# A conv-attention-MLP block on one core: pass 1 of the feed-forward part with its bias on TensorE, maxima taken from PSUM, and the normalisation on GpSimd

## The reference, cut to what matters

```python
def _quantize_activations_groupwise(x):      # 5 groups of 32 // 5 = 6 images, the last 2 images stay zero
    for g in range(5):
        ag = x[g * gs:(g + 1) * gs]
        gamma = jnp.max(jnp.abs(ag))
        xq = xq.at[g * gs:(g + 1) * gs].set(jnp.clip(ag * 128 / (gamma + 1e-5), -128 + 1e-5, 128 - 1e-5))
def _bitlinear(x, W, b):
    y = jnp.einsum('btc,oc->bto', x, binarized(W)) + b
    return _quantize_activations_groupwise(y)
h = _bitlinear(ln(t), W1, b1)                # 192 -> 768
out = _bitlinear(gelu(h), W2, b2)            # 768 -> 192
t = t + out
```

## Time and profile before

| | |
|---|---|
| time, median of 3 runs | 4890.53 us (4886.1 to 4891.87) |
| the profiled execution's own time | 4894.14 us |
| its span in the trace | 4892.3 us |
| PE busy | 4119.3 us (84% of the span) |
| DVE busy | 3418.6 us (70%) |
| ACT busy | 2759.7 us (56%) |
| POOL busy | 359.1 us (7%) |
| pass 1 of group 0: first statistics to last maximum | 785.92 to 895.42 us, 109.5 us |
| in it: PE, DVE, ACT, POOL busy | 75.84, 77.71, 58.63, 31.28 us |

### The profile page before, as it was taken

One profiled execution on the slowest core, in us unless ns is written; L12 is line 12 of the kernel. 1 busy time (PEld: TensorE's weight loads), 2 busy tenths in 40 slices (PEclk: granted clock), 3 DMA queues, 4 the chain that ended last, 5 costly groups with the idle time before them and its releaser, 6 DMA issues.

```text
span 4892.3 us, 114220 instructions
## 1 busy us (share of the span) xinstructions
PE 4119.3 (84%) x38848; PEld 2965.8 (61%) x38848; DVE 3418.6 (70%) x6624; ACT 2759.7 (56%) x5791; POOL 359.1 (7%) x311
## 2 busy tenths in 40 slices
PE   3989897879898878989887879889878989887878
PEld 2766664566676636766664566666536667664565
DVE  3767677777676667767677777676677767676776
ACT  1555555646565555555555655555565555565655
POOL 0000002000000120000002000000120000002000
PEclk8999998999999989999998999999989999998999
DMA  2111111011121101111111011121101111111011
GB/s 60 40 34 34 34 40 27 0 47 34 34 54 40 34 0 39 34 34 34 35 40 27 0 47 34 41 53 34 34 0 40 34 34 34 40 34 27 0 40 40
DMA packets 46377, 161.59 MB, mean 33 GB/s; under 512 B 10098, under 2 KB 10612, under 8 KB 45684
## 3 DMA queue, kind: packets, MB, share of 16 engines
q1 hardware_dynamic: 45812, 154.38, 13.3%
HBM read 28.52 MB, written 25.17 MB: 11 GB/s over the span
## 4 chain that ended last, share of the span: by engine, by line
issue 76%; PE 13%; POOL 6%; DVE 2%; ACT 2%; DMA 0%; POOLq 0%; SPq 0%; ACTq 0%; DVEq 0%
PE S L685 5%; PE PT L754 4%; POOL hi_z L478 2%; POOL hi_z L497 1%; POOL rstd L473 1%; POOL rstd L493 1%; ACT work L908 1%; POOL NK L468 1%; PE PT L649 1%; PE OUT L669 1%; DVE work L364 0%; DVE nmax L1103 0%; DMA B<-in_b 0%; PE S L635 0%; PE S L693 0%
## 5 line engine op out<-in xcount | busy, mean ns | idle before, releaser
L863 ACT ACTIVATE work<-S,nmax 128x256 f32<-128x256 f32 (+7 forms) x1536 | 1141.4, 744 | 1113.6 <-DVE nmax L1103 1048.5
L1103 DVE TENSOR_REDUCE nmax<-S 128x1 f32<-128x256 f32 (+7 forms) x1536 | 1157.4, 754 | 845.8 <-PE S L637 830.0
L649 PE MATMUL PT<-ident,work 128*128 128x128 f32 x6912 | 1112.7, 281 | 214.2 <-DVE work L364 184.4
L649 PEld LDWEIGHTS PT<-ident,work 128*128 128x128 f32 x6912 | 748.0, 142 | 430.5 <-DVE work L364 260.4
L364 DVE COPY work<-PT 128x512 f32<-128x512 f32 (+3 forms) x1536 | 893.5, 583 | 57.4 <-PE PT L649 52.3
L685 PE MATMUL S<-odd,W1b 128*128 (+1 forms) x2160 | 567.2, 419 | 96.0 <-ACT work L908 47.0
L685 PEld LDWEIGHTS S<-odd,W1b 128*128 128x128 f16 x2160 | 215.2, 106 | 419.8 <-issue 148.6
L635 PE MATMUL S<-KS,QS 128*128 128x512 f16 (+3 forms) x1152 | 333.1, 345 | 105.7 <-issue 57.0
L867 ACT ACTIVATE work<-PT 128x512 f32<-128x512 f32 (+3 forms) x768 | 331.8, 432 | 53.4 <-PE PT L649 53.4
L637 PE MATMUL S<-causal,identb 128*128 128x128 bf16 x1536 | 342.4, 223 | 0.0
L635 PE MATMUL S<-odd 128*128 128x512 f16 (+3 forms) x1152 | 315.1, 328 | 16.9 <-ACT work L863 14.8
(11 more groups left out here) (183 smaller groups left out, 5760.9 us busy)
## 6 DMA issues: line engine op xcount, KB each, us to landing
X<-in_x SPq DMA_DIRECT2D x32, 768.0 KB, 5.4
odd<-hi_z SPq DMA_DIRECT2D x128, 192.0 KB, 4.3
odd<-odd SPq DMA_DIRECT2D x128, 192.0 KB, 4.3
out_y<-work SPq DMA_DIRECT2D x64, 384.0 KB, 3.7
QS<-hi_z SPq DMA_DIRECT2D x64, 192.0 KB, 3.7
QS<-odd SPq DMA_DIRECT2D x64, 192.0 KB, 4.2
KS<-hi_z SPq DMA_DIRECT2D x64, 192.0 KB, 4.7
KS<-odd SPq DMA_DIRECT2D x64, 192.0 KB, 4.6
```

Of the source, the lines that this page charges most:

```text
L649: last = tr(bank[:, P * (j - c0):P * (j - c0) + P], PS[m % 2][:, m // 2 % 2, P * j:P * j + P], ident[:, :])
L863: A(PS[n % 2][:, n // 2 % 2, 0:w], S[:, n % 2, 0:w], ACT.Exp, bias=nmax[:, n % MAXES:n % MAXES + 1], accum_out=rowsum[:, sum_col(n):sum_co ...
L1103: v.tensor_reduce(nmax[:, n % MAXES:n % MAXES + 1], S[:, n % 2, 0:P * (qtile(n) + 1)], AX.X, ALU.max, negate=True).then_inc(max_made, 1)
```

## The change

In pass 1 only:

1. **Bias on TensorE.** The bias is cut once, in the setup, into three bf16 parts whose sum is the fp32 value; they stand in rows 0, 64 and 96 of an otherwise zero 128x768 array `B1S` (three DMAs of 768 single elements each into rows of `BF`, a view of `T1`; three operations of VectorE make the parts after image 0's front). Each product of 512 columns now starts with one more matmul, `B1S` against a bf16 column of ones read 512 times, and the three products add to it.
2. **Maximum of absolute values straight from PSUM.** VectorE reads the 1024 columns of `S` itself, with the absolute value applied; ScalarE's L891 and the array `JUNK` are gone, and TensorE waits for VectorE's maximum of block m-2 before it writes block m.
3. **Transposes between the tiles.** The four steps of `turn_z2(b + 1)` stand behind blocks 1, 2, 3 and 4 of `y1(b)`.
4. **Normalisation on GpSimd, rounding on ScalarE.** GpSimd does the eight subtract-and-scale operations of 128x192 (L510 of the new file), ScalarE the two roundings of 128x768 (`round_z2`), GpSimd again the two low parts. VectorE keeps the statistics and makes them two images ahead: those of image b+2 between the maxima of image b.

```diff
+            BF = T1[:, GS - 1, 0:4, :].rearrange("p t c -> p (t c)")
...
+            for row in (0, 64, 96):
+                sp.dma_start(BF[row:row + 1, :].rearrange("r (m p) -> r m p", m=MH), b1.rearrange("p m -> m p").unsqueeze(0),
+                             allow_slow_non_contiguous=True).then_inc(bias_parts_in, 16)
...  # GpSimd
-                with pool.Fori(0, GS) as b:
-                    ab = pool.snap(g * GS + b)
-                    pool.wait_ge(ln2_step, ab * LN_PER + 16)
+                for b in range(GS):
+                    ab = g * GS + b
+                    pool.wait_ge(ln2_step, ab * 16 + 16)
                     pool.tensor_tensor(rstd[:, :], mv[:, :, 1], epst[:, :], ALU.add).then_inc(rstd2_made, 1)
                     pool.wait_ge(rstd2_made, ab * 2 + 1)
                     pool.tensor_tensor(rstd[:, :], rstd[:, :], halfneg[:, 0:TT], ALU.pow).then_inc(rstd2_made, 1)
+                    pool.wait_ge(rstd2_made, ab * 2 + 2)
+                    alone(pool)
                     for hf in range(2):
-                        pool.wait_ge(ln2_step, ab * LN_PER + (25 + hf))
+                        pool.wait_ge(z2_rounded, ab * 2 + (hf + 1))
+                        alone(pool)
+                        for t in range(4 * hf, 4 * hf + 4):
+                            pool.tensor_scalar(Z[:, t, :], T1[:, b, t, :], mv[:, t, 0:1], rstd[:, t:t + 1], ALU.subtract,
+                                               ALU.mult).then_inc(z2_normed, 1)
+                    for hf in range(2):
+                        pool.wait_ge(z2_rounded, ab * 2 + (hf + 3))
                         ts = slice(4 * hf, 4 * hf + 4)
                         pool.tensor_tensor(zcat[:, ts, C:2 * C], Z[:, ts, :], zcat[:, ts, 0:C],
                                            ALU.subtract).then_inc(z2lo_made, 1)
...  # TensorE
-                        pe.wait_ge(abs_made, ab * MH + (m + 1))
+                        pe.wait_ge(max1_step, ab * MH + g + (m + MH - 1))
+                        alone(pe)
                         for hf in range(2):
-                            last = ffn1(Z2[:, b, hf], S[:, m % 2, 512 * hf:512 * hf + 512], m)
+                            bank = S[:, m % 2, 512 * hf:512 * hf + 512]
+                            mm(bank, B1S[:, P * m:P * m + P], onesb[:, :].broadcast_to([P, 512]), start=True, stop=False)
+                            for j in range(3):
+                                last = mm(bank, W1b[:, j, P * m:P * m + P], Z2[:, b, hf, j, :], start=False, stop=(j == 2))
                         last.then_inc(y1_full, 1)
+                        if ab1 is not None and 1 <= m <= 4:
+                            turn_z2(ab1, m - 1)
...  # ScalarE
+                def round_z2(ab):
+                    act.wait_ge(z2t_full, ab * 4 + 4)
+                    for hf in range(2):
+                        act.wait_ge(z2_normed, ab * 8 + (4 * hf + 12))
+                        alone(act)
+                        A(zcat[:, 4 * hf:4 * hf + 4, 0:C], Z[:, 4 * hf:4 * hf + 4, :], ACT.Copy).then_inc(z2_rounded, 1)
...
-                        A(JUNK[:, m, :], S[:, m % 2, :], ACT.Abs, bias=B1[:, m:m + 1]).then_inc(abs_made, 1)
...
+                with act.Fori(0, GS) as b:
+                    ab = act.snap(g * GS + b)
+                    round_z2(ab)
+                    put_z2(b, ab)
...  # VectorE, setup
+            dve.wait_ge(bias_parts_in, 48)
+            tops = BF.bitcast(BF16).rearrange("p (n two) -> p n two", two=2)[:, :, 1]
+            link(v.tensor_tensor(BF[64:P, :], BF[64:P, :], tops[64:P, :], ALU.subtract))
+            link(v.tensor_tensor(BF[96:P, :], BF[96:P, :], tops[96:P, :], ALU.subtract))
+            link(v.tensor_copy(B1S[:, :], tops))
...  # VectorE, pass 1
-                        v.tensor_reduce(gm1[:, b, m:m + 1], JUNK[:, m, :], AX.X, ALU.max).then_inc(max1_step, 1)
...
+                def aggregate2(ab):
+
+                    dve.wait_ge(z2_normed, ab * 8 + 8)
+                    dve.wait_ge(ln2_step, ab * 16 + 8)
...
+                    v.tensor_reduce(gm1[:, b, m:m + 1], S[:, m % 2, :], AX.X, ALU.max,
+                                    apply_absolute_value=True).then_inc(max1_step, 1)
...
+                with dve.Fori(0, GS - 2) as b:
                     ab = dve.snap(g * GS + b)
...
+                    for m in range(MH):
+                        max_y1(b, ab, m)
+                        if m == 1:
+                            dve.wait_ge(ln2_step, ab * 16 + 32)
+                            alone(dve)
+                        if 1 <= m <= 2:
+                            stats2(dve.snap(b + 2), range(4 * m - 4, 4 * m))
+                        if m == 3:
+                            aggregate2(dve.snap(ab + 2))
```

More of the change, by code:

```diff
@@ L303, in hybrid_kernel @@
         y1_full = sem("y1_full")
[L304 removed]
+        z2_normed = sem("z2_normed")
+        z2_rounded = sem("z2_rounded")
+        bias_parts_in = sem("bias_parts_in")
         max1_step = sem("max1_step")
@@ L707, in group_tail, with turn_z2, y1 @@
                 alone(pe)
[L709 to L717, removed]
+                def turn_z2(ab, k):
+                    if k % 2 == 0:
+                        pe.wait_ge(z2lo_made, ab * 2 + (k // 2 + 1))
+                    if k >= 2:
+                        pe.wait_ge(z2t_made, ab * 4 + (k - 1))
+                    turn_z(ZP[k % 2], k).then_inc(z2t_full, 1)
+                def y1(b, ab, ab1):
                     for m in range(MH):
@@ L885, in put_z2 @@
                           ACT.Copy).then_inc(z2t_made, 1)
-                def abs_y1(ab):
-                    for m in range(MH):
-                        act.wait_ge(y1_full, ab * MH + (m + 1))
-                        act.wait_ge(max1_step, ab * MH + g + (m + 1))
-                        A(JUNK[:, m, :], S[:, m % 2, :], ACT.Abs, bias=B1[:, m:m + 1]).then_inc(abs_made, 1)
-                put_z2(0, g * GS)
-                with act.Fori(0, GS - 1) as b:
+                with act.Fori(0, GS) as b:
                     ab = act.snap(g * GS + b)
-                    abs_y1(ab)
-                    put_z2(act.snap(b + 1), act.snap(ab + 1))
-                abs_y1(g * GS + (GS - 1))
+                    round_z2(ab)
+                    put_z2(b, ab)
                 act.wait_ge(quant1_step, (g + 1) * 4)
@@ L1121, in group_tail @@
                     dve.wait_ge(st, nb * (GS * STACKS) + STACKS)
-                def norm2(b, ab, part, tiles):
-                    layer_norm(lambda t: T1[:, b, t, :], ln2_step, ab * LN_PER, rstd2_made, ab * 2 + 2, part, tiles)
-                def max_y1(b, ab, ms):
-                    for m in ms:
-                        dve.wait_ge(abs_made, ab * MH + (m + 3))
-                        v.tensor_reduce(gm1[:, b, m:m + 1], JUNK[:, m, :], AX.X, ALU.max).then_inc(max1_step, 1)
-                halves = (range(4), range(4, 8))
@@ L1132, in group_tail @@
-                for part, tiles in (("stats", range(TT)), ("norm", range(TT)), ("round", halves[0]), ("round", halves[1])):
-                    norm2(0, g * GS, part, tiles)
-                with dve.Fori(0, GS - 1) as b:
-                    ab = dve.snap(g * GS + b)
-                    b1, ab1 = dve.snap(b + 1), dve.snap(ab + 1)
-                    norm2(b1, ab1, "stats", range(TT))
-                    max_y1(b, ab, range(2))
-                    dve.wait_ge(z2t_full, ab * 4 + 4)
-                    alone(dve)
-                    norm2(b1, ab1, "norm", range(TT))
-                    norm2(b1, ab1, "round", halves[0])
-                    norm2(b1, ab1, "round", halves[1])
-                    max_y1(b, ab, range(2, MH))
@@ L1146, in group_tail, with stats2 @@
-                max_y1(GS - 1, g * GS + (GS - 1), range(MH))
+                def stats2(b, tiles):
+                    for t in tiles:
+                        v.bn_stats(stats[:, t, :], T1[:, b, t, :]).then_inc(ln2_step, 1)
+                def aggregate2(ab):
+                    dve.wait_ge(z2_normed, ab * 8 + 8)
+                    dve.wait_ge(ln2_step, ab * 16 + 8)
+                    alone(dve)
+                    for t in range(TT):
+                        v.bn_aggr(mv[:, t, :], stats[:, t, :]).then_inc(ln2_step, 1)
@@ new lines, in max_y1 @@
+                def max_y1(b, ab, m):
+                    dve.wait_ge(y1_full, ab * MH + (m + 1))
+                    alone(dve)
+                    v.tensor_reduce(gm1[:, b, m:m + 1], S[:, m % 2, :], AX.X, ALU.max,
+                                    apply_absolute_value=True).then_inc(max1_step, 1)
+                for b in range(2):
+                    if b:
+                        dve.wait_ge(ln2_step, g * (GS * 16) + 16)
+                    stats2(b, range(TT))
+                    aggregate2(g * GS + b)
@@ L1147, in group_tail @@
+                for b in range(GS - 2, GS):
+                    for m in range(MH):
+                        max_y1(b, g * GS + b, m)
                 dve.wait_ge(max1_step, nb * (GS * MH) + g + MH)
```

32 lines of the change are left out of this document (19 added, 13 removed).

## The result

The changed kernel is slower: 5008.38 us, median of 4 runs (5003.43 to 5010.5), against 4889.48 us for the kernel before on the same chip. The ratio is 1.0242, with an interval of 1.0225 to 1.026. The prediction said 4815 us and a range of 4778 to 4862. The profiled execution's span is 5006.3 us, 114.0 more than before.

What follows compares the result with a forecast made beforehand. A chain across engines set pass 1's period; GpSimd's loop would now set it at 13.3 us. Gaining 15.5 us a group, 77 in five, turns 4894.14 into 4817, as a median about 4815 us, range 4778 to 4862.

Steps and rivals of the forecast that it cites:

- the price x: Pass 1: one 128x192 subtract-and-scale on GpSimd, taken as 0.40 us, eight per image, 3.2 us in the period.
- the case past the turning point: GpSimd's normalisation so dear, x from about 0.79 us, that the gain is used up; chance 0.08.
- the rival's 4933 us: Whole time if GpSimd's operation is dear: x = 1.0 us, each group losing 8.5 us, five 42; chance 0.08.
- waits of 1.5 us at most: TensorE's forecast wait before each image's first transposes, assumed to leave full clock after the first 12 matmuls.
- rival with a dear GpSimd: Pass 1: the two scalars make GpSimd's operation dear, TensorE waits at every image's first transposes; 4933 us at x = 1.0; chance 0.08.
- the clock stays low: Rival: waits keep TensorE at its lower clock throughout pass 1, 22.6 us an image, about 5020 us; chance 0.03.
- The setup: VectorE's three added operations, at most 3.5 us, hidden in its idle time, and three DMAs landing in time: both 0.
- the loop and its order: Pass 1: maximum, aggregation, `rstd`, eight normalisations, low part, first transposes, then blocks to block 3: 10.1 + 8x = 13.3 us.
- TensorE's 11.8 us an image: Pass 1: six blocks of 1.73 us and four transpose steps of 0.34 us, if nothing waits.
- VectorE's 10.1: Pass 1, per image: six maxima of 1.22 us, statistics 2.17, aggregation 0.64; less than TensorE's work, so no bound.
- ScalarE's 4.9: Pass 1, per image: two roundings and four copies at 0.81 us each, staying hidden.
- the rival with TensorE as the bound: Pass 1: GpSimd cheap or aggregation early, so TensorE's 11.8 us set the period; 4781 us; chance 0.17.

Runs made afterwards that it cites:

- norm_act: Changed kernel with the eight subtract-and-scale operations on ScalarE and VectorE's statistics and aggregation one block earlier: 4810.55 us, ratio 0.9832 to the kernel before.
- norm_act_late: `norm_act` with the three bias transfers of the setup issued only when weights and first image have landed: 4809.73 us, ratio 0.9833.
- pool_price_quiet: Kernel before plus one scratch GpSimd operation of each kind, issued once VectorE's setup is done; two scalar columns at 192 columns took 1.01 us.
- norm_dve: Changed kernel with the eight subtract-and-scale operations back on VectorE, between its maxima: 4839.72 us, ratio 0.9885 to the kernel before.
- pool_wide: Changed kernel with GpSimd's eight normalisations replaced by four two-tensor operations of 128x768 an image, with broadcast operands: 4955.5 us, ratio 1.0127.
- norm_dve_early: `norm_dve` with statistics, aggregation and normalisations each one block earlier: 4843.13 us, ratio 0.9896.
- act_block: `norm_act` with the four transpose steps in one piece behind block 5 instead of between the blocks: 4925.61 us, ratio 1.0061.

## Why the prediction was wrong

**The step that failed** is the price x of "eight normalisations: 8x". I took 0.40 inside bounds of 0.32 and 0.54, from GpSimd's one-input and two-tensor operations. It is 0.99 start to start, outside both. The bounds were those of other forms: each holds for its own, and neither has scalar columns. The row that I gave to the rival alone, 1.64 us for a power of 8 columns, was the hint that GpSimd's cost goes by the form. I gave the case past the turning point 0.08 with "subtract and multiply are as plain as the addition". The Trainium skill, "GPSIMD Engine Reference", section 4.1 (Engine selection), sends this work to VectorE, and the runs agree with that advice (4840 us on VectorE, 5008 on GpSimd); its figure of about line rate for one input doesn't hold for this form (1.01 us, where VectorE took 0.30).

From the start of the statistics to the one-column reduction I had 879.7 - 785.9 = 93.8 us, and it took 132.1. The 38.3 us are made up so:

- 8 x 0.59 = 4.7 us of price at the start and in each of four periods: 23.6 us. This alone, in five groups, is the rival's 4933 us.
- Half clock behind each of four waits: 4 x 2.06 = 8.2 us.
- Image 1: its low part came 2.1 us after TensorE was ready, where I had it 2.1 ahead, and behind this wait the half clock came once more (0.51 from 820.40 to 823.80), some 1.9 us: 4.0 us.
- The rest, 2.5 us, in handovers: 0.9 at the start, 0.3 a period, 0.4 at the end.

**The clock** was my second miss, and it hangs on the first. I assumed full clock behind waits of 1.5 us at most. The wait was 6.3 us, and behind it the clock was 0.50 for 4.5 us. My own rival with a dear GpSimd had the right mechanism and lacked this term: of the 75 us by which the result is above it, this makes up to 50 (10.1 us, the half clock behind image 1's wait included, in five groups). The rival "the clock stays low" came near the time (5020) by another way: the clock was 0.83 over a period and 1.00 at its end.

**The setup** at 0 was wrong by some 3 us: not VectorE's three operations, but the transfers, which held up the weights. Of the 5.75 us by which pass 1 started late, these are shown to be 2.7 at the first attention scores, and 3.5 at the start of the statistics (789.96 in `norm_act`, 786.45 in `norm_act_late`). The eight traces with the early transfers start there at 788.04 to 792.52, `before`, `norm_act_late` and `pool_price_quiet` at 785.92 to 786.49. So the rest is no more than the scatter among traces that have the same code up to that point.

**What was right:** the loop and its order; TensorE's 11.8 us an image with the added matmul at 0.216 (11.81 busy in `norm_act`, and a spacing of 0.21 to 0.22 between its neighbours); VectorE's 10.1 (9.9 to 10.0); the 1.22 us from PSUM; ScalarE's 4.9. With x out of the way, the rival with TensorE as the bound nearly came about: `norm_act`'s period is 12.17 us for 11.8. Its time is 4810 for 4781. Of these 29 us, 4.0 are the late first pass and 2.7 the pass of group 0 (89.85 us for 87.1). Some 3 us are the chip: the kernel before took 4893.2 us beside `norm_act`. The later groups gain 17.1 us each over the kernel before, by the reduction's starts, where group 0 gains 19.5 and the rival had 22.2; why they gain less isn't settled.

## What to carry to other kernels

A bound from neighbouring rows is one only if the operation has the same form: engine, operation and kinds of operands. Where everything hangs on a price that no row shows, the case "several times dearer" deserves a chance like that of the forecast, and its time must include what the wait does to TensorE's clock behind it. Before moving work to an engine because its share of the span is small, put its whole chain into the period of the stage; here ScalarE, at 56% of the span before, was the better place than GpSimd at 7%.

## What the runs showed of the hardware

- GpSimd, 192 columns of f32: a copy 0.34 us, two tensors 0.59, one constant 0.70, one scalar column 0.76 (one operation each); two constants 0.86, two scalar columns 1.01 (two operations). Why scalars and constants are dearer than a second tensor isn't shown.
- A VectorE operation of 192 columns with two scalar columns (0.37 us) took 1.70 us when it met GpSimd's two-tensor operation of 768 columns (1.59 us) in `norm_dve`; VectorE, not GpSimd, lost the time.
- A matmul of 512 columns whose moving operand is one column read 512 times costs as much as its neighbours: 0.21 to 0.22 us at full clock and 0.42 to 0.43 at half.
- Behind a wait of 6.3 us TensorE ran at 0.50 for 4.5 us, and the same behind the wait of 4.55 us in `pool_wide`. With the short waits of `norm_act`, `norm_dve` and `norm_dve_early` (up to 1.7 us) its clock was 1.00 all the period. In between the length alone doesn't tell: half clock followed waits of 1.83 us (`act_block`, 840.62) and 2.10 us (the changed kernel, image 1 of group 0), and full clock one of 3.23 us (the same image in group 4, clock 1.00 from 4563.11 to 4567).
- Three transfers of 768 single elements (3 KB each), issued at 7 us behind the weights' and the input's, put VectorE's first work on the weights back from 20.07 to 22.26 us; issued at 21.6 (`norm_act_late`) they cost nothing that the trace shows.
